# Summing the odd states from 7 on in the other half of y, joined by one transfer, with every place in the order moved

## The reference, cut to what matters

```python
def step(h, inputs):
    dt, bt, ct, xt_ = inputs
    decay = jnp.exp(A[None] * dt[:, :, None])
    inp = dt[:, :, None] * xt_[:, :, None] * bt[:, None, :]
    h = decay * h + inp
    y = jnp.einsum('bdn,bn->bd', h, ct)
    return (h, y)
...
return jnp.einsum('bld,ed->ble', y * gate, Wo) + bo
```

## Time and profile before

| | us |
|---|---|
| median of 3 runs (1943.89 to 1952.47) | 1944.59 |
| the profiled execution, its own time | 1943.78 |
| its span in the trace | 1942.0 |
| PE busy | 1722.2 (89%) |
| DVE busy | 1679.5 (86%) |
| ACT busy | 1401.2 (72%) |
| POOL busy | 931.0 (48%) |

### The profile page before, as it was taken

One profiled execution on the slowest core, in us unless ns is written; L12 is line 12 of the kernel. 1 busy time (PEld: TensorE's weight loads), 2 busy tenths in 40 slices (PEclk: granted clock), 3 DMA queues, 4 the chain that ended last, 5 costly groups with the idle time before them and its releaser, 6 DMA issues.

```text
span 1942.0 us, 31131 instructions
## 1 busy us (share of the span) xinstructions
PE 1722.2 (89%) x9620; PEld 1005.9 (52%) x9620; DVE 1679.5 (86%) x3928; ACT 1401.2 (72%) x2724; POOL 931.0 (48%) x693
## 2 busy tenths in 40 slices
PE   6989788999989898999989898999989898888875
PEld 2545444646555564646555564646455464535333
DVE  4653888999999999899999999999999899878793
ACT  3666768797886978687886878687886867675641
POOL 2000454555555555555555555555555455565431
PEclk9999899999999999999999999999999999999997
DMA  5322576977878686978878786877878686651110
GB/s 141 90 59 73 125 162 138 178 157 167 165 153 183 161 181 147 173 154 167 167 152 181 159 182 150 175 156 168 162 156 176 147 170 144 151 120 55 50 60 16
DMA packets 186086, 275.26 MB, mean 142 GB/s; under 512 B 33809, under 2 KB 125762, under 8 KB 185922
## 3 DMA queue, kind: packets, MB, share of 16 engines
q1 hardware_dynamic: 155682, 163.17, 33.7%
q0 software_dynamic: 30240, 110.11, 31.2%
HBM read 128.49 MB, written 34.08 MB: 84 GB/s over the span
## 4 chain that ended last, share of the span: by engine, by line
PE 39%; DVE 20%; ACT 12%; DMA 12%; issue 7%; POOL 6%; SPq 3%; POOLq 0%; DVEq 0%; ACTq 0%
DVE hc L1274 8%; PE bank L423 7%; DMA y<-hc 7%; PE bank L542 4%; DVE bank L1131 4%; PE bank L642 3%; DMA sk<-qk_parts 3%; PE bank L487 3%; PE bank L509 3%; SPq L852 3%; PE bank L434 3%; PE bank L625 2%; DVE hc L1282 2%; PE bank L417 2%; POOL inp L1447 2%
## 5 line engine op out<-in xcount | busy, mean ns | idle before, releaser
L1447 POOL TENSOR_TENSOR inp<-u,b_all 128x1024 f32<-128x1024 f32 x240 | 577.0, 2404 | 366.7 <-DVE hc L1274 183.4
L1274 DVE TENSOR_TENSOR_SCAN hc<-dec,inp 128x1024 f32<-128x1024 f32 x256 | 586.8, 2292 | 51.9 <-POOL inp L1447 16.8
L1131 DVE CUSTOM_DVE_ANT_0 bank<-bank,mask_qk 128x512 f32<-128x512 f32 (+3 forms) x1024 | 479.6, 510 | 83.7 <-PE bank L487 83.1
L916 ACT ACTIVATE pt<-bank 128x512 f32<-128x512 f32 x640 | 380.6, 606 | 83.0 <-PE bank L525 53.2
L1032 ACT ACTIVATE dec<-dt,a_neg 128x511 f32<-128x511 f32 x512 | 339.6, 729 | 33.5 <-DVE hc L1274 33.3
L1456 POOL DMA_DIRECT2D y<-hc x210 | 186.1, 886 | 339.2 <-DMA y<-hc 295.0
L1282 DVE TENSOR_TENSOR hc<-hc,bank 128x1024 f32<-128x1024 f32 x242 | 294.1, 1215 | 17.5 <-PE bank L679 16.5
L487 PE MATMUL bank<-sk,sq 96*128 96x512 bf16 (+3 forms) x1024 | 249.9, 305 | 34.0 <-DVE mall L1131 19.8
L509 PE MATMUL bank<-sq,sk 98*128 98x512 bf16 (+3 forms) x1024 | 249.0, 304 | 28.1 <-ACT pt L916 24.0
L542 PE MATMUL bank<-pt,v_sb 128*32 128x512 f32 (+3 forms) x2048 | 181.0, 451 | 8.1 <-ACT pt L916 7.4
L487 PEld LDWEIGHTS bank<-sk,sq 96*128 96x128 bf16 x1024 | 94.6, 99 | 158.7 <-issue 58.3
(11 more groups left out here) (169 smaller groups left out, 3022.0 us busy)
## 6 DMA issues: line engine op xcount, KB each, us to landing
y<-hc POOLq DMA_DIRECT2D x210, 512.0 KB, 5.4
b_all<-b_kept SPq DMA_DIRECT2D x256, 256.0 KB, 3.9
qk_parts<-parts SPq DMA_DIRECT2D x96, 256.0 KB, 3.0
sq<-qk_parts SPq DMA_DIRECT2D x384, 64.0 KB, 3.7
sk<-qk_parts SPq DMA_DIRECT2D x384, 64.0 KB, 3.8
X<-in_x SPq DMA_DIRECT2D x16, 512.0 KB, 7.3
out<-X SPq DMA_DIRECT2D x16, 512.0 KB, 3.3
sq<-hlt SPq DMA_DIRECT2D x256, 2.0 KB
```

Of the source, the lines that this page charges most:

```text
L916: A(pt[:, n % PT, :], score_bank[unit % 2][:, :], ACT.Exp).then_inc(exp_done.sem, 1)
L1131: return V.tensor_tensor_reduce(src[:, o:o + n], src[:, o:o + n], mask_qk[:, T - n:T], 1.0, -3.0e38, ALU.add, ALU.max, out)
L1274: V.tensor_tensor_scan(h, d, v, 0.0, ALU.mult, ALU.add).then_inc(scan_done.sem, 1)
L1447: G.tensor_tensor(inp[:, n % 2, :, :], u[:, :, :], b_all[:, k % 3, None, :].to_broadcast([P, C, T]), ALU.mult).then_inc(inp_ready.sem, 1)
```

## The change

The state after which the second half is used is called `SECOND` (7). The product of state 7 is written into the other half of y and needs no addition. The additions of states 9, 11 and 13 (`BESIDE`) go to that half, each behind the one before in it. The others (1 to 6, 8, 10, 12, 14, 15) go to the batch's own half. `merge_y` adds the other half to the own one, after the additions of 13 and of 14 have landed and before the addition of 15. A batch has 15 such transfers in both kernels.

```diff
+    SECOND = 7
+    BESIDE = (9, 11, 13)
+    AFTER_MERGE = 15
+    OWN_SUM = tuple(n for n in range(1, NS) if n != SECOND and n not in BESIDE)
...
+        def own_turn(n):
+            return OWN_SUM.index(n) + (n >= AFTER_MERGE)
...
-        y_added = tally("y_added", NS - 1, 16)
+        y_added = tally("y_added", len(OWN_SUM) + 1, 16)
+        y_beside = tally("y_added_beside", len(BESIDE), 16)
...
-                elif old_n == 0:
-                    dve.wait_ge(hc_done.sem, hc_done.at(old_s, 1))
+                elif old_n in (0, SECOND):
+                    dve.wait_ge(hc_done.sem, hc_done.at(old_s, old_n + 1))
+                elif old_n in BESIDE:
+                    dve.wait_ge(y_beside.sem, y_beside.at(old_s, BESIDE.index(old_n) + 1))
                 else:
-                    dve.wait_ge(y_added.sem, y_added.at(old_s, old_n))
+                    dve.wait_ge(y_added.sem, y_added.at(old_s, own_turn(old_n) + 1))
...
-                V.tensor_tensor(hc[:, k % HC, :, :] if n or s >= LATE else y[:, s % 2, :, :], hc[:, k % HC, :, :],
+                dst = hc[:, k % HC, :, :]
+                if s < LATE and n == 0:
+                    if s:
+                        dve.wait_ge(y_added.sem, y_added.at(s - 1))
+                    dst = y[:, s % 2, :, :]
+                if s < LATE and n == SECOND:
+                    if s:
+                        for c in range(C):
+                            dve.wait_ge(side["turn", 1, c].free, side["turn", 1, c].at("turn", s - 1, 1, c))
+                    dst = y[:, (s + 1) % 2, :, :]
+                V.tensor_tensor(dst, hc[:, k % HC, :, :],
                                 spread_bank[:, None, :].to_broadcast([P, C, T]), ALU.mult).then_inc(hc_done.sem, 1)
...
-                if n > 1:
-                    pool.wait_ge(y_added.sem, y_added.at(s, n - 1))
-                pool.dma_start(y[:, s % 2, :, :], hc[:, (NS * s + n) % HC, :, :],
-                               accum_op=ALU.add).then_inc(y_added.sem, 16)
+                if n in BESIDE:
+                    half, added, turn = (s + 1) % 2, y_beside, BESIDE.index(n)
+                else:
+                    half, added, turn = s % 2, y_added, own_turn(n)
+                if turn:
+                    pool.wait_ge(added.sem, added.at(s, turn))
+                pool.dma_start(y[:, half, :, :], hc[:, (NS * s + n) % HC, :, :],
+                               accum_op=ALU.add).then_inc(added.sem, 16)
+
+            def merge_y(s):
+                pool.wait_ge(y_beside.sem, y_beside.at(s))
+                pool.wait_ge(y_added.sem, y_added.at(s, own_turn(AFTER_MERGE) - 1))
+                pool.dma_start(y[:, s % 2, :, :], y[:, (s + 1) % 2, :, :], accum_op=ALU.add).then_inc(y_added.sem, 16)
```

Beside this nearly every number in the five tables and in `OWN` is another, most by 1 to 5 half steps. Two lines of POOL's table stand for them:

```diff
-               "add": (160, 152, 162, 174, 175, 182, 185, 190, 199, 209, 212, 214, 219, 221, 223, 228)}
+               "add": (160, 156, 160, 170, 174, 179, 188, 190, 202, 206, 210, 217, 217, 223, 224, 228), "merge": 226}
```

More of the change, by code:

```diff
@@ L105, in hybrid_block @@
             "gate": (0, 1), "bc": 1, "dt": (0, 0), "x3": (1, 0), "turn1": (0, 1), "low1": 1, "hw1": 0, "up1": (0, 1)}
-    ACT_AT = {"res": (-32, -29), "square_f": 98, "square_s": 125, "square_l": 251, "norm_f": 101, "norm_s": 129,
[5 rows of a table removed]
-              "decays": (157, 163, 168, 169, 171, 172, 179, 188, 198, 204, 204, 213, 214, 217, 223, 227)}
-    DVE_AT = {"gated": 247, "add_x3": (249, 250), "in0": 111, "in1": 265, "out0": 117, "out1": 269,
-              "add_up1": (278, 279), "add_x1": (96, 94), "add_up0": (122, 125), "silu": 145, "delta": 154,
-              "stats_q": -110, "finish": -9, "heads": 26,
-              "scan": (160, 167, 169, 171, 177, 184, 192, 196, 201, 205, 211, 214, 218, 225, 229, 232),
-              "product": (168, 170, 172, 177, 182, 190, 195, 199, 203, 210, 211, 215, 222, 228, 230, 237)}
@@ new lines, in hybrid_block @@
+    DVE_AT = {"gated": 247, "add_x3": (249, 250), "in0": 113, "in1": 265, "out0": 116, "out1": 269,
+              "add_up1": (278, 280), "add_x1": (94, 94), "add_up0": (123, 125), "silu": 144, "delta": 153,
+              "stats_q": -110, "finish": -9, "heads": 26,
+              "scan": (160, 167, 169, 171, 176, 184, 192, 198, 201, 206, 211, 215, 219, 224, 227, 231),
+              "product": (168, 170, 173, 176, 180, 190, 195, 200, 204, 209, 212, 218, 221, 226, 229, 234)}
+    POOL_AT = {"rsqrt_f": 81, "rsqrt_s": 121, "rsqrt_q": -114, "rsqrt_l": 238, "low": (108, 258),
+               "inputs": (147, 156, 156, 156, 159, 161, 172, 182, 190, 200, 204, 208, 213, 217, 218, 224),
+               "add": (160, 156, 160, 170, 174, 179, 188, 190, 202, 206, 210, 217, 217, 223, 224, 228), "merge": 226}
@@ L123, in hybrid_block @@
+    SP_AT = {"parts": (-38, 2), "load_x": -113, "store_b": 149, "store": 282, "stack": (-31, -31, -31), "maxima": -7,
+             "load_b": (152, 158, 158, 159, 171, 173, 180, 183, 195, 202, 206, 210, 212, 215, 219, 225)}
     OWN = {
         1: {
[7 rows of a table removed]
-                   "sum": (136, 151, 160, 164, 165, 173, 174, 186, 189, 196, 202, 202, 218, 219, 225, 225)},
-            "ACT": {"res": (-51, -42), "square_f": 92, "square_s": 127, "norm_f": 98, "norm_q": -106, "norm_l": 254,
[4 rows of a table removed]
-                   "decays": (154, 157, 163, 167, 168, 180, 182, 190, 197, 202, 205, 210, 215, 219, 225, 228)},
@@ L139, in hybrid_block @@
-            "DVE": {"gated": 246, "in0": 109, "in1": 268, "out0": 112, "out1": 270, "add_up1": (278, 278),
-                   "add_x1": (90, 90), "add_up0": (124, 128), "silu": 143, "delta": 152, "stats_q": -100,
-                   "scan": (159, 165, 166, 171, 180, 184, 190, 201, 202, 207, 211, 215, 219, 226, 227, 230),
-                   "product": (161, 165, 169, 179, 181, 190, 196, 201, 205, 208, 213, 220, 222, 228, 231, 233)},
-            "POOL": {"rsqrt_f": 99, "rsqrt_s": 123, "rsqrt_q": -94, "rsqrt_l": 237, "low": (117, 260),
-                   "inputs": (135, 141, 151, 152, 158, 171, 172, 183, 195, 201, 205, 208, 210, 214, 215, 225),
-                   "add": (160, 155, 160, 171, 179, 180, 193, 199, 206, 207, 210, 214, 214, 225, 226, 227)},
@@ new lines, in hybrid_block @@
+            "ACT": {"res": (-56, -43), "square_f": 89, "square_s": 125, "norm_f": 92, "norm_s": 128, "norm_q": -109,
[4 rows of a table added]
+                   "decays": (153, 155, 163, 164, 168, 178, 187, 188, 190, 202, 208, 208, 214, 216, 221, 229)},
+            "DVE": {"gated": 246, "in0": 110, "in1": 268, "out0": 112, "add_up1": (278, 281), "add_x1": (87, 89),
+                   "add_up0": (122, 126), "silu": 145, "stats_q": -87,
+                   "scan": (155, 159, 164, 171, 177, 184, 187, 201, 202, 206, 213, 214, 219, 224, 227, 232),
+                   "product": (162, 166, 169, 175, 182, 189, 194, 201, 202, 207, 213, 218, 220, 229, 230, 234)},
@@ L1506, in _ @@
                 for a, n in steps(now, POOL_AT["add"]):
-                    if n and a < LATE:
+                    if a < LATE and n not in (0, SECOND):
                         add_state(a, n)
+                if 0 <= (a := due(now, POOL_AT["merge"])) < LATE:
+                    merge_y(a)
 def kernel(**inputs):
```

73 lines of the change are left out of this document (39 added, 34 removed), and 88 rows, old and new, of tables (ACT_AT, OWN, PE_AT).

## The result

The changed kernel takes 1955.09 us (median of 12 runs, 1951.81 to 1963.09), the kernel before 1944.24 (12 runs, 1935.54 to 1952.47). The ratio is 1.0064, with a 95% interval of 1.0048 to 1.0081: slower by 0.5 to 0.8%, where 1942 and "no change" were forecast. The profiled execution took 1954.6 us, span 1952.8.

The account below looks back on a forecast made before the run. DVE, 93.3% busy, and what it waits for were taken to set the pace. From the profiled 1943.8 us, terms of -12, +14 and -4 gave 1941.8, forecast as 1942 us, no change (1934.9 to 1954.3); 8 in 10: 1918 to 1964.

Parts of the forecast that it names:

- term 3: All places moved: new places change DVE's waits for PE; a gain of 4 us, 15 either way.
- term 1: Late additions wait for the one two states earlier, shortening scan waits: gain 18 us, 12 let through.
- term 2: Additions 14, merge, 15 end late for the gate: 1.5 us in each of 14 batches, 21 us, 14 let through.
- the two thirds: Share of terms 1 and 2 let through to the time, since a delayed DVE finds PE further ahead.
- (a): Rival, faster: the end chain is in time at the gate, 1917 us or 1925; chance 0.28.
- (b): Rival, slower: the gate waits 2.9 us in each of 14 batches, 41 us, giving 1969 us; chance 0.22.
- (c): Rival: POOL's waits shrink but no wait of DVE moves, 1939.8 us; chance 0.36 together with the forecast.
- (d): Rival: the new places alone decide, by more than 10 us either way; chance 0.14.

Follow-up runs that it names:

- the old places: Tables of the kernel before, put under the changed structure: 1961.99 us with the merge, 1927.63 us without it.
- one chain: Kernel before (15 additions to one half) with the changed kernel's tables, addition 7 of batch 0 moved to 195: 2007.32 us.
- the first run: Changed structure, merge included at 226, with every table of the kernel before, against the kernel before: 1961.99 us.

## Why the prediction was wrong

**The step that failed is the sum: three terms, each taken as if it held whatever the others were, and in it term 3.** -12 + 14 - 4 came to -2; +10.9 was measured. The merge was priced for the order of the changed kernel ("the changed queue holds one unit of 256 twice more"), and in its places the merge adds 8.3 us where 14 was forecast, while relief and places together give +2.6 where -16 was. There terms 1 and 3 are off by 18.6 us, more than the whole miss of 12.9, and term 2 by 5.7 the other way. Counted the other way, with the old places first, the relief gives 16.9, the merge takes 36.6 and the places give 8.8, and the miss looks like one of term 2. Both ways of counting are right; the 28.3 us between them is what the prediction had no term for.

**Term 3.** "No row prices them. I take a gain of 4 us ... with 15 either way". The new places are worth -8.8 us with the merge, +19.5 without it and +65.0 with one chain. The working looked only at DVE's waits for PE (L498 and L690), and these fell by 12.3 us, more than it hoped. It left out what the places do to everything else that DVE waits for. The scans of states 8 to 15 wait 15.6 us in batches 1 to 13, against 10.6 before and 4.0 with the split in the old places, and `dt` waits 7.2 us against 0.9 before. The new places keep the merge's price low, at 8 to 10 us, and pay for that in these waits.

**Term 1, the relief, was right in the old places, in part by luck, and no third of it was lost.** Taken at 18, let through at 12, measured at 16.9. Its explanation covers less: before, the scans of states 8 to 15 waited only 10.6 us in batches 1 to 13, not 18, and 6.6 of it went; the head is 5.2 us shorter, and the rest is spread over DVE's waits in the frames. What I named as its sign, L1287 below 8 us, did not come: in the changed kernel these scans wait 26.0 us. By state, 9.1 of it is at 11 and 5.4 at 5, and it stays without the merge (9.1 and 5.1), so it belongs to the new places.

**Term 2.** "I take 1.5 us for each of 14 batches: 21 us", of which 14 were let through. The gate's wait itself was not taken too small: it is 18.4 us in the old places and 10.0 in the changed kernel. The chain of three took 17.2 us in the batch shown of the first run and 17.5 in that of the changed kernel, between three medians (16.2) and the 18.15 of its own rows of before. What was wrong stood beside it. The input of the next state 0 was priced at nothing "as long as addition 14 lands within some 6.6 us"; in the old places the merge started 7.6 us after addition 14, and state 0's scans waited 15.1 us against 6.8 without a merge. In the changed kernel addition 14 is in time, and they wait 1.8. And the two thirds: DVE's 17 + 2 us of joining cost 20, 39 us more of waits cost 37, and only for half a merge can some of the 16.8 us have been lost.

**The rivals.** (a) fell with its condition: the gate does wait. (b) has 1969, and the split in the old places took 1962, but that is luck: the gate waited 18.4 us there and not 41, and the rest came from state 0 and from what no trace shows. (c) fell: the relief moves DVE. (d) is not cleanly decided: with the merge the places give 8.8 us, under its 10, and without it they cost 19.5.

**The checks named.** POOL's landings under 150 us: 147. The gate waiting 1.5 us in most batches: ten of 14, 1.0 us each. DVE's waits for L498 and L690 differing from 39.9 by more than 15 if (d): 27.6, a difference of 12. But it was not slack that shrank at no cost: about the same amount now stands at the gate and at `dt`. Time from before the first gate or after the last: the head gives 2.6 us and the tail takes 3.3 of the 10.8, so most of it lies between the gates.

**Still open.** Where the 10 us behind batch 9 come from is not settled; they are there without the merge too (444.9 us for the four frames, against 440.0, and 204.4 for the tail, against 197.5), and putting the tables of before there made them worse. Nor is the part of term 1 that lies outside the late scans, nor whether the loads of `b_all` make the slow link of the chain. Of the ways to join the halves that were tried, none beats the kernel before: the best, on DVE, is at 1948.0. The relief is real, and each of them gives it back.

## What to carry to other kernels

Splitting a chain of accumulations pays in its middle and is paid for at its end: price the join by what waits for its end, and also by what else stands behind it in the queue that issues it (18.4 and 8.3 us here). Where one engine is 93% busy, a microsecond ahead of an instruction that it cannot pass was here nearly a microsecond of the program; don't discount it by a third without a row that says so. Places that were searched for a structure belong to that structure, and a change that brings both has to be taken apart with the cross of the two before any of it is explained.

## What the hardware showed that was not expected

A GpSimd instruction that reads two tiles and a DVE instruction that reads two tiles did not share in these runs: the second stood still. u took 3.25 us instead of 1.22 beside POOL's join, POOL's join 3685 ns instead of 2355 beside DVE's work, and scan and `inp`, let go at the same time, 2700 and 2823 ns in the mean instead of 2287 and 2407. An accumulating transfer of half the size, 256 KB, lands in 3.3 us against 4.5 in the same place (medians of 14; in other places the merge of 512 KB has medians up to 6.4), so by an estimate from these two about 2.1 us of the time to landing do not shrink with size (3.3 - 1.2). The Trainium skill (DMA: Bandwidth & Descriptors, Anatomy of one DMA) has a fixed part of about 2.0 us, which agrees; its 436 GB/s for the rest do not, since 256 KB in 1.2 us are 218 GB/s.
